# Rotary attention: the low halves of the TensorE-turned weights are made by VectorE out of PSUM

## The reference

```python
    q = input_embeds @ Wq.T + bq
    k = input_embeds @ Wk.T + bk
    v = input_embeds @ Wv.T + bv
    ...
    q, k = _apply_rope(q, k)
    scores = jnp.einsum('bhqd,bhkd->bhqk', q, k) * scale
    attn = jax.nn.softmax(scores, axis=-1)
    out = jnp.einsum('bhqk,bhkd->bhqd', attn, v)
    out = out.transpose(0, 2, 1, 3).reshape(B, S, NUM_HEADS * HEAD_SIZE)
    return out @ Wo.T + bo
```

## Time and profile before

| | |
|---|---|
| median of three runs | 2741.61 us (2740.38 to 2743.81) |
| profiled execution: its own time | 2743.55 us |
| profiled execution: span of the trace | 2741.8 us |
| mean granted TensorE clock | 0.945 |
| attention stage, first to last score maximum | 693.7 to 1341.2 us |
| a whole inner unit of 8 steps | 40.8 us |
| busy over the span: PE / DVE / ACT / POOL | 87% / 72% / 55% / 67% |

### The profile page before, as it was taken

One profiled execution on the slowest core, in us unless ns is written; L12 is line 12 of the kernel. 1 busy time (PEld: TensorE's weight loads), 2 busy tenths in 40 slices (PEclk: granted clock), 3 DMA queues, 4 the chain that ended last, 5 costly groups with the idle time before them and its releaser, 6 DMA issues. The chain is left out here.

```text
span 2741.8 us, 56038 instructions
## 1 busy us (share of the span) xinstructions
PE 2399.0 (87%) x21310; PEld 1556.0 (57%) x21310; DVE 1981.8 (72%) x3620; ACT 1503.8 (55%) x2069; POOL 1837.6 (67%) x1732
## 2 busy tenths in 40 slices
PE   6887787886899999999789999998788799999986
PEld 3555544644566676666556666665534466666655
DVE  7998545446677777777488888886286888888862
ACT  4222122322788888888625665556452256665564
POOL 1888100000999999999637899999610388999985
PEclk9899788988899999999889999999888999999998
DMA  1000000002689998899615555555411055555554
GB/s 44 1 1 0 0 23 13 1 23 64 123 159 161 151 157 162 150 153 163 118 49 90 96 93 95 95 95 97 76 31 53 20 99 94 93 93 93 95 102 80
DMA packets 763819, 226.74 MB, mean 83 GB/s; under 512 B 745992, under 2 KB 754696, under 8 KB 763552
## 3 DMA queue, kind: packets, MB, share of 16 engines
q1 hardware_dynamic: 763552, 223.16, 44.8%
HBM read 20.70 MB, written 1.05 MB: 8 GB/s over the span
## 5 line engine op out<-in xcount | busy, mean ns | idle before, releaser
L2275 PE MATMUL banks<-g_w,normed_t 128*128 128x320 f32 x1536 | 512.2, 460 | 42.2 <-DVE g_scratch L2580 38.3
L1575 POOL TENSOR_TENSOR g_p_lo<-g_p,g_p_hi 128x512 bf16<-128x512 f32 (+1 forms) x256 | 416.0, 1645 | 43.3 <-POOL g_z L2469 21.6
L1764 DVE TENSOR_REDUCE at_negmax<-banks 128x1 f32<-128x1024 f32 x256 | 301.5, 1219 | 154.6 <-PE banks L1676 154.6
L2275 PEld LDWEIGHTS banks<-g_w,normed_t 128*128 128x128 f32 x1536 | 265.7, 192 | 224.0 <-issue 81.0
L1741 POOL TENSOR_TENSOR at_p_lo<-at_p,at_p_hi 128x640 bf16<-128x640 f32 x256 | 356.0, 1407 | 13.2 <-ACT at_p_hi L1729 11.4
L1588 DVE TENSOR_REDUCE g_negmax<-banks 128x1 f32<-128x1024 f32 x256 | 310.3, 1217 | 32.8 <-PE banks L1499 30.4
L1565 ACT CAST g_r_hi<-banks 128x512 bf16<-128x512 f32 x128 | 74.9, 585 | 427.7 <-PE banks L1510 427.7
L1552 ACT ACTIVATE g_p<-banks,g_negmax 128x1024 f32<-128x1024 f32 x256 | 285.1, 1114 | 9.6 <-DVE g_negmax L1588 8.3
L1722 ACT ACTIVATE at_p<-banks,at_negmax 128x1024 f32<-128x1024 f32 x256 | 285.4, 1115 | 6.3 <-DVE at_negmax L1764 6.3
L1676 PE MATMUL banks<-at_k_t,at_q 64*128 64x512 f32 x1024 | 258.0, 623 | 18.5 <-POOL at_k_t L2025 9.7
L1499 PE MATMUL banks<-g_k_t,g_q 64*128 64x512 f32 x1024 | 254.4, 615 | 12.3 <-ACT g_p L1552 6.3
(11 more groups left out here) (414 smaller groups left out, 6327.3 us busy)
## 6 DMA issues: line engine op xcount, KB each, us to landing
at_swapped<-at_crossed SPq DMA_DIRECT2D x128, 128.0 KB, 2.8
g_w<-in_ex_w SPq DMA_DIRECT2D x2, 2880.0 KB, 11.5
f_w<-in_W SPq DMA_DIRECT2D x2, 1024.0 KB, 5.6
at_rope<-in_rope SPq DMA_DIRECT2D x1, 2048.0 KB, 9.8
at_t_hi<-at_p_hi SPq DMA_TRANSPOSE x128, 3.6
at_t_lo<-at_p_lo SPq DMA_TRANSPOSE x128, 3.6
g_t_hi<-g_p_hi SPq DMA_TRANSPOSE x128, 4.0
g_t_lo<-g_p_lo SPq DMA_TRANSPOSE x128, 3.8
```

What stands on the lines that cost most here:

```text
L1575: self.nc.gpsimd.tensor_tensor(self.part(self.p_lo, j, h), self.p[:, j % 2, h, 0:self.WIDTH[h]], self.part(self.p_hi, j, h), ALU.subtract) ...
L1764: self.nc.vector.tensor_reduce(self.negmax[:, j % 2, h:h + 1], self.core.banks[:, first:first + 2, :], AX.XY, ALU.max, negate=True).then_i ...
L2275: nc.tensor.matmul(out[:, 0:ED], core.xt[:, at:at + P], w[:, kind * H + tile // (T * BATCH) * 2 + h, :], start=True, stop=True).then_inc(p ...
```

## The change

`u_lo` is no longer made by GpSimd out of `u` but by VectorE, straight out of the PSUM banks in which the turned blocks stand. The new method is `dve_split`, in the place of `pool_split`. `scores` of j+1 now waits until `u_split` of j-1 has come, in the place of `u_copied`: the banks are held until VectorE has read them too. VectorE does the split of step j-1 at the head of its step j, ahead of the maxima of j+1, and that of the last step at the end. `dve_split` still waits for the copy, because `u_hi` comes from it.

```diff
@@ scores
         if j >= 2:
-            pe.wait_ge(self.u_copied, j - 1)
+            pe.wait_ge(self.u_split, j - 1)
@@
-    def pool_split(self, pool, j):
-        pool.wait_ge(self.u_copied, j + 1)
+    def dve_split(self, dve, j):
+        dve.wait_ge(self.u_copied, j + 1)
         if j >= self.RING:
-            pool.wait_ge(self.av_done, j - self.RING + 1)
-        self.nc.gpsimd.tensor_tensor(self.u_lo[:, j % self.RING], self.u[:, j % self.RING], self.u_hi[:, j % self.RING],
-                                     ALU.subtract).then_inc(self.u_split, 1)
+            dve.wait_ge(self.av_done, j - self.RING + 1)
+        self.nc.vector.tensor_tensor(self.u_lo[:, j % self.RING].rearrange("p g n -> p (g n)"), self.spent(j),
+                                     self.u_hi[:, j % self.RING].rearrange("p g n -> p (g n)"), ALU.subtract).then_inc(self.u_split, 1)
@@ GpSimd's loop over the steps
                 for h in range(2):
                     hs.pool_lo(pool, j, h)
-                hs.pool_split(pool, j)
@@ VectorE's loop over the steps
             for j in range(STEPS):
                 unit, t = j // hs.T, j % hs.T
+                if j:
+                    hs.dve_split(dve, j - 1)
                 if j + 1 < STEPS:
                     for h in range(2):
                         hs.dve_max(dve, j + 1, h)
@@ behind that loop
+            hs.dve_split(dve, STEPS - 1)
             for j in range(STEPS - hs.LAG, STEPS):
                 hs.dve_normalise(dve, j)
```

## The result

The changed kernel takes 2992.77 us in the median of four runs (2989.88 to 2996.37) against 2742.71 us, a ratio of 1.0913 with a 95% interval of 1.0894 to 1.0932. That is 250 us more; the forecast was 2966 us, inside a range of 2930 to 3025. The profiled execution took 2993.25 us with a span of 2991.5, against 2743.55 and 2741.8.

A forecast was written before the change was run, and what follows sets the result against it. TensorE's full queue, not GpSimd, was taken as the bound. Inner units +206, last +6 and first +12 us gave +224: 2743.6 became 2968, less 1.9 us to the median 2966 us, range 2930 to 3025.

The forecast's parts named there:

- What bounds the kernel before: Attention stage: TensorE's gapless queue sets the pace, 40.37 of 40.83 us busy; freeing GpSimd alone can't shorten such a step.
- a rotation step: Attention steps t = 0 to 3, rotations on VectorE: 7.03 us foreseen from maxima to maxima, against 4.83 before.
- the 0.46 us per unit of the forecast: TensorE's idle time per inner attention unit, the most it could gain from a freed GpSimd; at most 7 us over 16 units.
- The removed splits bring nothing: 128 splits of 1.469 us leave GpSimd, 188.0 us busy; the forecast took no gain for it.
- The split's price: VectorE's added 768-column subtraction out of PSUM, one per step: taken as 0.95 us, with ends 0.82 and 1.22.
- The ring: VectorE and TensorE each idle while the other works, scores waiting for VectorE's split: unit 55.5 us against 40.83; 81%.
- the handover: From the end of VectorE's split to the start of TensorE's scores: 0.06 us in each step.
- The clock: Rival: TensorE's clock halves after idle stretches, scores 3.78 us; +76 us (3042) if a third of steps fell; 12%.
- the ring's own range: 2936 to 3013 us: split between 0.82 and 1.22 gives -17 to +34 us, three handovers +-13.
- The sum: Attention stage: +206 us for fourteen inner units, +6 for the last, +12 for the first, together +224 us.
- The hidden wait: Rival: copy and split end at 955.8, just before the scores of 955.97, so no change; 2741 us, 4%.
- The other signs that had been named: Profile after: split 0.95 us; steps 7.0, 7.1, 6.6; TensorE waits some 220 us; GpSimd about half, waiting for ScalarE.

The follow-up runs named there:

- The filled kernel: Changed kernel plus nine more f32 transposes of the identity per step on TensorE, ahead of the wait for the split; 2969.09 us, ratio 1.0828.

## Why the prediction was right, point by point

**What bounds the kernel before: right.** TensorE's queue was full. The run with short GpSimd instructions shows it from the other side: GpSimd at 12.53 of 40.84 us, and the unit as long as before. GpSimd's 98% had been no bound. That kernel carries VectorE's split too, whose list was put at 4.86 us in a rotation step, so it doesn't show what a relief of GpSimd alone would bring; the 0.46 us per unit of the forecast remain the ceiling for that.

**The removed splits bring nothing: right, as far as it was tried.** No kernel came below the kernel before.

**The split's price: right.** 0.954 was worked out between the 640 and the 1024 columns; it took 0.947.

**The ring: right in its members, a little short in one.** Measured, in a rotation step: 2.27, 1.32, 0.19, 0.21 and 0.95, within 0.01 of the forecast, then 0.14 for the handover where 0.06 was put, and 1.99 to the maxima (1053.41 to 1055.40) where 2.02 was. That gives 7.07 against 7.03; the steps t = 4, 5 took 7.17 against 7.09, t = 6, 7 took 6.68 against 6.60, a unit 56.0 against 55.5. Over 14 units this is 7 us. The mis-sized term is the handover, whose row of 0.06 came from the first layer. The length of the idle time ahead is not what makes it longer. In the kernel with the split behind the maxima the scores come 0.14 us behind the split too (961.34 + 0.95 = 962.29), after only 0.46 us of idle time, while the earlier trace rows had 0.57 us of idle time and a handover of 0.06:

```profile
962.43 1.99 PE L1676 MATMUL banks<-at_k_t,at_q 64*128 64x512 f32 x8 [0.46 <-DVE at_u_lo L1748]
```

What goes with it in the traces is how TensorE waits. `scores` has two waits, for the exponential and for the split, and the changed kernel has a semaphore instruction of 0.051 us for the second one ahead of the weights of the scores. The view of its line:

```profile
L1672 PEldq EVENT_SEMAPHORE  x126: 51/51/51, 701.6 to 1590.2; - x126
```

The filled kernel has none there: its fillers take the wait for the exponential, and the weight load of the scores waits for the split itself. That this instruction is the cause was not tried by itself.

**The clock: the one rival that came true, in part.** It was put outside the ring, with 12% and at +76 us if a third of the steps fell. It fell in some of the steps t = 0 to 4, most of them rotation steps, and the fourteen inner units took 804.3 us, which is 20.3 above 14 times 56.0. The row that spoke for a steady clock had one idle stretch of 2.5 us in it; here 2.18 us came back in every rotation step. One of the prediction's own marks of being wrong, scores that take longer than 2.0 us, was met in these steps (3.59 us above). The result lies even inside the ring's own range of 2936 to 3013, but that room had been kept for the split's price and the handovers, not for the clock. The ring with a few falls would have been 2986 us in the place of 2966.

**The sum.** 224 foreseen, 7 of handover and 20 of clock make 251, against 250 measured, and the last microsecond of that is luck. The stage alone grew by 254.7 us (693.7 to 1341.2 before, 691.2 to 1593.4 after): 232.7 in the fourteen inner units, and 22 in the first and last unit, where 18 had been put. The rest of the program, which is the same in both kernels, took 5 us less in this execution.

**The hidden wait: rightly turned down.** This case had been given 4% because VectorE has the maxima, the rotations and the normalising ahead of the split. The three kernels that move only the split (2903, 2785, 2762 us) come nearer to its 2741 step by step: what is taken from between the scores and the split leaves the step, as long as TensorE's own work is not longer. None of them reaches it.

The other signs that had been named were all seen: the split on VectorE at 0.95, the three step lengths, 219.6 us of waits of TensorE for `at_u_lo` where some 220 had been put, and GpSimd at 52% of a unit and waiting for ScalarE's high halves.

## What to carry to other kernels

When a wait of the fullest engine is moved to a later event, write down the list of the engine that produces this event, and see whether any instruction ahead of it waits for the fullest engine itself. If so, the two make a ring, and its length is the plain sum of the durations on the way, whatever the busy shares say. The place of the split in VectorE's list was worth 208 of 250 us here. With the bank not held, the split on VectorE cost 27 us beside a busy GpSimd, and 3 once GpSimd's instructions were short.

## What the runs showed of the hardware

- VectorE's subtraction of 768 columns took 0.945 to 0.959 us out of PSUM in the five kernels that do it so, whatever GpSimd did beside it. With both inputs in SBUF it took 1.44 us in the median and up to 2.34 beside GpSimd, and 0.95 in the median once most of GpSimd's instructions were short. The read out of PSUM, which holds the bank, is also what keeps the two engines apart: a version that gives up the one pays by the other.
- TensorE's clock fell to its half 16 times in the fourteen inner units, in steps t = 0 to 4, most of them rotation steps with idle stretches of 2.18 us that come every 7 us, and never in the steps t = 6 and 7 with stretches of about 1.5 us. With the split ahead of the normalising (idle for 1.78 us) it still fell now and then (six of the 56 rotation steps of the inner units took 8.2 to 8.3 us in the place of 6.67), and with the split behind the maxima (idle for 0.4 us) not at all. Nine small transposes in each idle stretch kept it at 2.4 GHz.
- A handover from VectorE to TensorE took 0.14 us where a semaphore instruction of TensorE carried the wait, after 2.18 us of idle time as after 0.46, and 0.05 us where the weight load waited by itself.
